# Layer norm statistics, router products and one input transform of a fused conv, attention and router kernel, rearranged in its first two stages

## The reference

```python
xn = _layernorm(x, axis=-1)                      # eps 1e-5, no weights
# attention branch
x = conv_general_dilated(xn, conv_w, 'SAME') + conv_b      # 3 taps, 4096 -> 3072
q, k, v = split(x, 3)                            # blocks of 128 tokens, 16 heads of 64
...                                              # causal softmax within a block
s = (o @ wo + bo) @ proj_w + proj_b
# router branch
scores = softmax(xn @ router_weight.T + router_bias)       # 64 experts
topk_w, topk_idx = top_k(scores, 8)
ffn = xn * topk_w.sum() + w_dense @ expert_bias
out = inputs + s * silu(ffn)
```

## Time and profile before

| | us |
|---|---|
| median of 3 runs | 1282.74 |
| range of the runs | 1281.09 to 1283.9 |
| profiled execution, its own time | 1284.49 |
| its span (slowest core, core 4) | 1283.0 |
| spans of the eight cores | 1272.1 to 1283.0 |
| PE busy in the span | 1089.1 |
| VectorE busy | 719.6 |
| ScalarE busy | 429.5 |
| GpSimd busy | 115.8 |

### The profile page before, as it was taken

The page is one execution under the profiler, slowest core; times in us unless marked ns, Lnnn a source line. Parts: engine busy times, 40 slices in busy tenths (PEclk is TensorE's granted clock), DMA queues, the critical chain, the costliest instruction groups (busy, mean ns, idle before and its releaser), DMA issues.

```text
span 1283.0 us, 15540 instructions; the slowest of 8 cores (1272.1 to 1283.0 us)
## 1 busy us (share of the span) xinstructions
PE 1089.1 (85%) x5200; PEld 493.9 (38%) x5200; DVE 719.6 (56%) x1140; ACT 429.5 (33%) x688; POOL 115.8 (9%) x128
## 2 busy tenths in 40 slices
PE   0119999999899998999999999999971555699997
PEld 0104444444344443444444444444430333433332
DVE  1877787677566525666665456666411444445454
ACT  1673333333233233333332433333212555322221
POOL 0002221000000000000000000000400000034544
PEclk9999999999899998999999999999995567799999
DMA  9910113667566548777776677777999000146765
GB/s 288 343 54 30 58 67 108 215 221 242 169 227 225 177 166 270 231 232 225 229 231 188 202 229 231 227 229 229 202 183 172 2 1 1 66 138 225 223 208 191
DMA packets 47943, 229.43 MB, mean 179 GB/s; under 512 B 6292, under 2 KB 6580, under 8 KB 44468
## 3 DMA queue, kind: packets, MB, share of 16 engines
q1 hardware_dynamic: 42872, 213.99, 52.8%
q0 software_dynamic: 3856, 13.27, 6.1%
q10 hardware_dynamic: 1136, 1.16, 0.3%
HBM read 222.79 MB, written 18.89 MB: 188 GB/s over the span
## 4 chain that ended last, share of the span: by engine, by line
PE 84%; DVE 7%; DMA 3%; issue 2%; another core or an unknown queue 2%; ACT 1%; ACTq 0%; POOLq 0%; DVEq 0%; SPq 0%
PE PS L202 80%; PE PS L206 4%; DVE AL L237 3%; DVE AL L209 2%; DMA AL<-rw 2%; DVE tNm L639 1%; DMA AL<-cw 1%; ACT AL L213 1%; ACTq L70 0%; DVE tMv L240 0%; ACT AL L215 0%; ACT tSd L213 0%; POOLq L804 0%; DVE tRr L658 0%
## 5 line engine op out<-in xcount | busy, mean ns | idle before, releaser
L202 PE MATMUL PS<-AL 128*128 128x512 bf16 (+4 forms) x4608 | 992.8, 379 | 20.6 <-DVE AL L209 15.2
L202 PEld LDWEIGHTS PS<-AL 128*128 128x128 bf16 (+3 forms) x4608 | 437.1, 102 | 551.9 <-issue 95.5
L209 DVE TENSOR_TENSOR AL<-AL 128x512 bf16<-128x512 f32 (+1 forms) x704 | 451.9, 687 | 265.8 <-PE PS L202 212.8
L213 ACT ACTIVATE AL<-AL 128x1024 bf16<-128x1024 f32 x193 | 203.4, 1054 | 426.9 <-PE PS L202 399.6
L206 PE MATMUL PS<-tI128f,AL 128*128 128x128 f32 (+3 forms) x304 | 43.2, 281 | 85.5 <-ACT AL L213 52.7
L209 POOL TENSOR_TENSOR AL<-AL 128x1024 f32<-128x1024 f32 x32 | 74.9, 2342 | 279.7 <-DVE AL L209 279.7
L213 ACT ACTIVATE AL<-PS 128x512 f32<-128x512 f32 (+2 forms) x88 | 56.5, 679 | 100.9 <-PE PS L206 77.2
L795 DVE SCALAR_TENSOR_TENSOR AL<-AL,tSc,PS 128x1024 f32<-128x1024 f32 x32 | 41.0, 1281 | 77.2 <-PE PS L202 77.2
L209 DVE TENSOR_TENSOR AL<-PS,AL 128x512 f32<-128x512 f32 (+1 forms) x80 | 71.9, 899 | 20.2 <-ACT AL L213 18.0
L206 PEld LDWEIGHTS PS<-tI128f,AL 128*128 128x128 f32 (+3 forms) x304 | 34.3, 152 | 109.1 <-issue 107.5
L213 ACT ACTIVATE AL<-AL,tScb 128x1024 f32<-128x1024 f32 x32 | 36.7, 1148 | 113.1 <-DVE AL L795 113.1
(11 more groups left out here) (52 smaller groups left out, 212.6 us busy)
## 6 DMA issues: line engine op xcount, KB each, us to landing
AL<-cw SPq DMA_DIRECT2D x192, 768.0 KB, 5.0
AL<-x SPq DMA_DIRECT2D x16, 1024.0 KB, 31.0
AL<-x SPq DMA_DIRECT2D x32, 512.0 KB, 4.9
out<-AL SPq DMA_DIRECT2D x32, 512.0 KB, 5.8
AL<-pw POOLq DMA_DIRECT2D x8, 1024.0 KB, 50.1
AL<-wq SPq DMA_DIRECT2D x8, 512.0 KB, 3.6
AL<-wk SPq DMA_DIRECT2D x8, 512.0 KB, 3.7
qhs<-AL SPq DMA_DIRECT2D x1, 2048.0 KB, 8.7
```

What stands on the lines that cost most here:

```text
L202: return PE.do(lambda e: e.matmul(out, lhsT, rhs, start=start, stop=stop, skip_group_check=skip), *toks, tok=tok)
L209: return eng.do(lambda e: e.tensor_tensor(out, a, b, op), *toks, tok=tok)
L213: return AC.do(lambda e: e.activation(out, in_, func, bias=bias, scale=scale), *toks, tok=tok)
```

## The change

It has five parts.

- **Loads.** The tiles are loaded in the order 0, 4, 1, 5, 2, 6, 3, 7, and the identity matrix has a semaphore of its own, so that the edge transposes no longer wait for the router weights.
- **Layer norm.** `ln_stats` is split into statistics, `ln_var` (aggregate and square root) and `ln_coef`. The square root of a tile is waited for only behind the first two `bn_stats` of the next tile. The square root is taken of 4(var + eps), so the reciprocal is `t_rh` itself and the halving is gone. The split of the projection bias, with its two DMAs on SyncE, stands behind the loop of stage 2.
- **Router.** The products of the odd tokens go to partitions 64 to 127 of the same bank instead of a bank of their own; the copy of the logits is one [128 x 512] instead of two [64 x 512], and its 8 transposes are 4 of 128 x 128.
- **Input transform.** Transform 0 of each chunk is made by GpSimd. Its token joins VectorE's in `k_v[c]`.
- **Conv units.** Pass 0 runs 4 matmuls in every step, from `st_` = 3, instead of 16 in every fourth; `prep` of unit g + 2 comes at `st_` = 4g + 3 instead of 4g + 5.

```diff
-        for t, d in ((t_i128f, d_i128), (t_cbT, d_cb), (t_bqT, d_bq), (t_bkT, d_bk),
+               for j in (0, 4, 1, 5, 2, 6, 3, 7)]
+        k_x = [k_x[i] for i in (0, 2, 4, 6, 1, 3, 5, 7)]
+        k_i128f = AC.dma(S("sC0"), t_i128f[:], d_i128)
...
+            return act(t_sd[rows, j:j + 1], t_mv[rows, 2 * j + 1:2 * j + 2], AF.Sqrt, k, k_eps,
+                       bias=t_eps[rows, :], scale=4.0)
+
+        def ln_coef(j, rows, k):
+            k = DV.do(lambda e: e.reciprocal(t_rh[rows, j:j + 1], t_sd[rows, j:j + 1]), k, tok=True)
...
-        k = act(t_pbh[:], t_pb[:], AF.Copy, k_c1)
-        k = tt(DV, t_pbl[:], t_pb[:], t_pbh[:], ALU.subtract, k)
-        SY.dma(S("sPB"), d_pbs[0], t_pbh[:], k)
-        k_pbs = SY.dma(S("sPB"), d_pbs[1], t_pbl[:])
-        k_edge = act(t_edge[:], PS[:, 0:64], AF.Identity, k_ed)
+                      k_xen, k_i128f, tok=(c == NCH - 1))
         all_r = slice(0, 128)
-        k_xn = []
-        for j in range(8):
-            k = ln_stats(j, xn[:, j, :], all_r, k_x[j])
-            k_xn.append(ln_apply(j, xn[:, j, :], all_r, k, 4))
+        k_xn = [None] * 8
+        k_sd = None
+        for i in range(8):
+            j = (i % 2) * 4 + i // 2
+            ln_stats(j, xn[:, j, :], all_r, k_x[j], 0, 2)
+            if i:
+                jp = ((i - 1) % 2) * 4 + (i - 1) // 2
+                k_xn[jp] = ln_apply(jp, xn[:, jp, :], all_r, ln_coef(jp, all_r, k_sd), 4)
+            k_sd = ln_var(j, all_r, ln_stats(j, xn[:, j, :], all_r, k_x[j], 2, 8))
+            if i == 1:
+                k_edge = act(t_edge[:], PS[:, 0:64], AF.Identity, k_ed)
+        k_xn[7] = ln_apply(7, xn[:, 7, :], all_r, ln_coef(7, all_r, k_sd), 4)
...
-                tt(DV, vout(3), h2(E0), h2(E1), ALU.subtract, k_p, tok=False)
-                k_v[c] = tt(DV, vout(0), h2(O0), h2(O1), ALU.subtract)
+                k_v0 = tt(GP, vout(0), h2(O0), h2(O1), ALU.subtract, k_ecopy, k_ocopy, k_p)
+                k_v[c] = (tt(DV, vout(3), h2(E0), h2(E1), ALU.subtract, k_p), k_v0)
...
-                mm(p_lg[:, 0:512], rwT[:, c, :], esb[i][:, 0:512], c == 0, c == NCH - 1,
-                   k_eo[c][0], k_c1)
-                k_rt[c] = mm(p_lg[:, 512:1024], rwT[:, c, :], osb[i][:, 1:513], c == 0, c == NCH - 1,
-                             k_eo[c][1], tok=True)
-                eo_free[i] = [k_v[c], k_rt[c]]
-            c = st_ - 2
-            if c >= 0 and c % 4 == 3:
-                g = c // 4
-                prep(g + LOOK)
-                k_pass[0] = conv_unit(g, 0, k_v)
+                mm(p_lg[0:64, :], rwT[:, c, :], esb[i][:, 0:512], c == 0, c == NCH - 1,
+                   k_eo[c][0], k_c1, skip=True)
+                k_rt[c] = mm(p_lg[64:128, :], rwT[:, c, :], osb[i][:, 1:513], c == 0, c == NCH - 1,
+                             k_eo[c][1], tok=True, skip=True)
+                eo_free[i] = [*k_v[c], k_rt[c]]
+            c = st_ - 3
+            if c >= 0:
+                if c % 4 == 0:
+                    prep(c // 4 + LOOK)
+                k_pass[0] = conv_unit(c // 4, 0, k_v, [c % 4])
...
-        k_lg = []
-        for h in range(2):
-            k_lg.append(DV.do(lambda e, h=h: e.tensor_scalar(
-                lgT[:, 512 * h:512 * h + 512], p_lg[:, 512 * h:512 * h + 512], 2.0, t_rbT[:],
-                ALU.mult, ALU.add), k_rt[NCH - 1], k_v[NCH - 1], tok=True))
-        k_lgfree = k_lg[1]
+        k = act(t_pbh[:], t_pb[:], AF.Copy, k_c1)
+        k = tt(DV, t_pbl[:], t_pb[:], t_pbh[:], ALU.subtract, k)
+        SY.dma(S("sPB"), d_pbs[0], t_pbh[:], k)
+        k_pbs = SY.dma(S("sPB"), d_pbs[1], t_pbl[:])
+
+
+        k_lgfree = DV.do(lambda e: e.tensor_scalar(lgT, p_lg, 2.0, t_rbT[:], ALU.mult, ALU.add),
+                         k_rt[NCH - 1], *k_v[NCH - 1], tok=True)
```

More of the change, by code:

```diff
@@ L99, in build_program @@
     d_pb = din("pb", [32, 128])
-    d_rb = din("rbT", [64, 1])
+    d_rb = din("rbT", [128, 1])
     d_i128 = din("i128", [128, 128])
@@ L166, in build_program @@
         osb = [f32v(B_KH + 4160 * i + 2080, 516) for i in range(2)]
-        lgT = f32v(B_KH, 1024, 64)
+        lgT = f32v(B_KH, 512)
         lgt = f32v(B_KH + 4096, 512)
@@ L220, in build_program @@
         k_x = [[SY.dma(S(f"sX{j}{h}"), xn[:, j, 2048 * h:2048 * h + 2048],
-                       d_x[j][:, 2048 * h:2048 * h + 2048]) for h in range(2)] for j in range(8)]
-        for t, d in ((t_i128f, d_i128), (t_cbT, d_cb), (t_bqT, d_bq), (t_bkT, d_bk),
+                       d_x[j][:, 2048 * h:2048 * h + 2048]) for h in range(2)]
+               for j in (0, 4, 1, 5, 2, 6, 3, 7)]
+        k_x = [k_x[i] for i in (0, 2, 4, 6, 1, 3, 5, 7)]
+        k_i128f = AC.dma(S("sC0"), t_i128f[:], d_i128)
+        for t, d in ((t_cbT, d_cb), (t_bqT, d_bq), (t_bkT, d_bk),
                      (t_bvT, d_bv), (t_boT, d_bo), (t_rbT, d_rb), (t_pb, d_pb)):
-            k_c1 = AC.dma(S("sC1"), t[:], d)
-        k_c1 = AC.dma(S("sC1"), rwT.rearrange("p c e -> p (c e)"), d_rw)
+            AC.dma(S("sC1"), t[:], d)
+        AC.dma(S("sC1"), rwT.rearrange("p c e -> p (c e)"), d_rw)
         k_c1 = (S("sC1"), S("sC1").n)
@@ L229, in build_program, with ln_stats @@
         k_c2 = (S("sC2"), S("sC2").n)
-        k_eps = DV.do(lambda e: e.memset(t_eps[:], EPS), tok=True)
-        def ln_stats(j, src, rows, loads):
+        k_eps = DV.do(lambda e: e.memset(t_eps[:], 4.0 * EPS), tok=True)
+        def ln_stats(j, src, rows, loads, c0, c1):
             s0 = 48 * j
             k = None
-            for c in range(8):
+            for c in range(c0, c1):
                 k = DV.do(lambda e, c=c: e.bn_stats(stats[rows, s0 + 6 * c:s0 + 6 * c + 6],
@@ L239, in ln_stats, with ln_var @@
                           loads[c * len(loads) // 8], tok=(c == 7))
+            return k
+        def ln_var(j, rows, k):
+            s0 = 48 * j
             k = DV.do(lambda e: e.bn_aggr(t_mv[rows, 2 * j:2 * j + 2], stats[rows, s0:s0 + 48]),
                       k, tok=True)
[L242 to L246, removed]
+            return act(t_sd[rows, j:j + 1], t_mv[rows, 2 * j + 1:2 * j + 2], AF.Sqrt, k, k_eps,
+                       bias=t_eps[rows, :], scale=4.0)
+        def ln_coef(j, rows, k):
+            k = DV.do(lambda e: e.reciprocal(t_rh[rows, j:j + 1], t_sd[rows, j:j + 1]), k, tok=True)
             return DV.do(lambda e: e.tensor_scalar(t_nmh[rows, j:j + 1], t_mv[rows, 2 * j:2 * j + 1],
@@ L260, in build_program @@
         r2 = slice(0, 2)
-        k = ln_stats(8, xe, r2, [k_xe])
-        k_xen = ln_apply(8, xe, r2, k, 1)[0]
+        k = ln_var(8, r2, ln_stats(8, xe, r2, [k_xe], 0, 8))
+        k_xen = ln_apply(8, xe, r2, ln_coef(8, r2, k), 1)[0]
         ed = PS[:, 0:64].rearrange("p (c s) -> p c s", c=NCH)
@@ L315, in dripped @@
                     drip.pop(0)()
-        p_lg = PS[0:64, 2048:3072]
+        p_lg = bank(4)
         bE, bO = bank(6), bank(7)
@@ L331, in h2, with conv_unit @@
             return a.rearrange("p (h f) -> p h f", h=2)
-        def conv_unit(n, setb, v_toks):
+        def conv_unit(n, setb, v_toks, ccs=range(4)):
             kind, p, g = stream[n]
@@ L337, in conv_unit @@
             k = None
-            for cc in range(4):
+            for cc in ccs:
                 c = 4 * g + cc
-                PE.wait(v_toks[c])
+                PE.wait(*v_toks[c])
                 for v in (1, 2, 3, 0):
@@ L344, in conv_unit @@
                            c == 0, c == NCH - 1, tok=(cc == 3 and v == 0))
-            u_free[u] = k
+            if 3 in ccs:
+                u_free[u] = k
             return k
@@ L413, in router_pe1 @@
             k = None
[L414 to L417, removed]
+            for j in range(4):
+                k = tr(pb_[:, 128 * j:128 * j + 128], lgT[:, 128 * j:128 * j + 128],
+                       t_i128f[:], k_lgfree, tok=(j == 3))
+            rd["k"] = DV.do(lambda e: e.tensor_copy(
+                lgt.rearrange("p (e j f) -> p j e f", e=2, j=4),
+                pb_.rearrange("p (j e f) -> p j e f", e=2, j=4)), k, tok=True)
             return rd["k"]
@@ L439, in r_keep @@
             k = tt(DV, t_wsum[:], ts8, rs8, ALU.mult, rd["k"])
-            k = tt(DV, t_sc[:], t_wsum[:], t_r[:, 0:8], ALU.mult, k)
+            k = DV.do(lambda e: e.scalar_tensor_tensor(t_sc[:], t_wsum[:], 2.0, t_rh[:, 0:8],
+                                                       ALU.mult, ALU.mult), k, tok=True)
             k = tt(DV, t_scb[:], t_sc[:], t_mv[:, 0:16:2], ALU.mult, k)
@@ L843, in _prep @@
         pb=cont(arr("L0_attn_proj_b").reshape(32, 128)),
-        rbT=cont(arr("L0_ffn_router_bias").reshape(64, 1)),
+        rbT=cont(np.tile(arr("L0_ffn_router_bias").reshape(64, 1), (2, 1))),
         i128=np.eye(128, dtype=f32),
```

4 lines of the change are left out of this document (1 added, 3 removed).

## The result

The changed kernel takes 1243.95 us (median, 1241.99 to 1244.83), the kernel before 1282.17 in the same runs: ratio 0.9698, 95% interval 0.9686 to 0.9711, 38.2 us less. The forecast was 1255 in 1243 to 1267, so the time lies at the fast edge of the range, nearer to the first rival (1246) than to the forecast. All times are medians over executions in which all eight cores ran at their usual granted clock (0.94 to 0.95 on the mean); in a few others half of the cores had 0.81 to 0.86, and those took over 1400 us.

A forecast was written before the change was run, and what follows sets the result against it. PE was taken to bound the kernel, after a VectorE-bound stage 1; in the changed loop VectorE with GpSimd. Stage 1's 23.3 us plus 5.3 from loop and handover (-7.4 + 2.1) gave 1254.1, forecast as 1255, range 1243 to 1267 (0.8).

The forecast's parts named there:

- the first rival: Steady loop: GpSimd and VectorE don't disturb each other, PE bounds at 3.3 us a step, 1246 us; chance 0.2.
- the prediction's own signs: Changed profile: prediction is wrong if the loop's step leaves 3.4 to 3.7 us or tiles land after 60 us.
- the later of the two limits: Stage 1: VectorE's eight tiles end at 59.3 us, loads plus four statistics at 60.5; the second ends last.
- the covered square root: Layer norm: the next tile's two statistics (1.2 us) cover the square root, even where it queues behind the normalising.
- even pass, even pass, odd pass, odd pass: only the second even and the first odd pass are neighbours: Router matmuls on PE: one of four passes is hidden, 0.45 us a step, so PE needs 3.3 us.
- the hold of 1.17 us: Steady loop: VectorE stands 1.17 us behind each GpSimd transform, middle of 1.08 to 1.26, giving 3.5 us a step.
- the sum (1254.1): Whole kernel: stage 1's 23.3 us plus loop and handover's 5.3 us, 28.6 us off, giving a median of 1254.1.
- unforeseen waits: Whole kernel: small waits only add, so the forecast was put at 1255 instead of 1254.1.
- a gap of 1 to 2 us ahead of pass 1 and 0.5 at unit 10: Handover: PE waits 1 to 2 us for the logits' copy; stores ahead of unit 10's loads cost 0.5 us more.

The follow-up runs named there:

- c_rw: The changed kernel with the router weights (1 MB) loaded on SyncE's queue behind the tiles instead of beside them: 1243.36 us, ratio 0.9691.
- b_bias: The kernel before with only the bias split moved behind stage 2's loop and the edge copy behind the tiles: 1262.75 us, ratio 0.9850.
- b_ln: The kernel before with all of the changed stage 1 and nothing of stage 2: 1264.26 us, ratio 0.9843.
- a_rser: The changed kernel with both router products on the first 64 columns and banks of their own, as before: 1263.55 us, ratio 0.9840.
- e_read: The changed kernel with GpSimd's transform on VectorE, edge copies on ScalarE, plus an unused two-input GpSimd read (f32 output) every step: 1272.19 us, ratio 0.9923.
- e_readb: The changed kernel with GpSimd's transform on VectorE, edge copies on ScalarE, plus an unused two-input GpSimd read (bf16 output) every step: 1270.51 us, ratio 0.9907.
- A: The changed kernel itself, with all five parts, against the kernel before: 1243.95 us, ratio 0.9698.

## Why the prediction was right or wrong

The time lies within the range, but by the prediction's own signs its working failed in two sizes: a step of 3.10 is outside of 3.4 to 3.7, and the last aggregate came at 64.10 instead of 60 to 61. The two errors have opposite signs, and only the width of the range, which was drawn to take in the first rival, covers what is left. That part was luck.

**Stage 1: right in its mechanism, 2 us too much.** VectorE started on tile 0 at 11.9 us, as said. (What held it before was not the bias split alone: the edge copy waited for the same weights.) The term that was mis-sized is "the later of the two limits": VectorE's 5.9 us a tile and the loads' 6.1 (2.1 MB at 345 GB/s) are so close that a late half costs time that is not made up. VectorE waited 6.7 us for halves; with 1 MB less ahead of them (c_rw) it waited 4.6 and ended earlier. The last product came at 64 to 66 instead of 62.0: 21 us instead of 23.3, and in the eight other kernels with this stage 1 the loop starts 19 us earlier. What I gave the moved statistics credit for, the covered square root, is worth nothing that can be measured (0.9850 in b_bias, 0.9843 in b_ln, and starts of 75.1 and 73.9, within the spread of equal stages).

**PE's step: wrong.** The step "even pass, even pass, odd pass, odd pass: only the second even and the first odd pass are neighbours" took the order of the instructions for the order of their four records. The records start in pairs; 0.85 to 0.9 us a step is hidden, not 0.45, and PE needs 2.85 instead of 3.3. The Trainium skill (TensorEngine Tiling (Array Packing), Theoretical Speedup), which gives up to twice the throughput, was right here, and I gave it too little weight. The error did not enter the forecast, since PE was not to be the bound. It would have mattered with the right hold: at 3.10 for the pair of VectorE and GpSimd, a PE of 3.3 would have set the step.

**VectorE with GpSimd: right mechanism, hold too large.** This pair sets the loop, as forecast. The term that was mis-sized is the hold of 1.17 us, the time that VectorE loses for each transform of GpSimd: 4 x 3.10 less 9.3 (12 x 0.60 + 2.1) is 3.1, or 0.77 for each transform. The step is 3.10 instead of 3.5, and the loop gives 0.64 x 31 = 20 us before the handover instead of 7.4. Less the 2.3 us of stage 1, that is the 10 us by which the sum (1254.1) was too slow; the eleventh is what the forecast of 1255 had added for unforeseen waits. In a_rser the same transform costs VectorE (77.13 - 93 x 0.60)/24 = 0.89, a read of other data 1.07 (e_read). All three rest on 0.60 for an operation of VectorE, and are good to about 0.1. Why the real transform is the cheapest was not found; the type of its output isn't it (e_readb).

**The first rival** (GpSimd and VectorE don't disturb each other, 1246) came nearest in number, with a mechanism that is shown false: the step was not PE's, PE waited, and taking GpSimd out gained 7 us.

**The handover: right in its mechanism.** Forecast were a gap of 1 to 2 us ahead of pass 1 and 0.5 at unit 10; 1.79 and, on the mean of the cores, 0.8 were there (1.38 on core 6). The first load behind the stores took 5.9 us to land instead of 5.2.

**The sum.** On the mean of the cores: -21.0 for the start and -15.9 from there to attention, against -36.9 in the spans. The time, that of the slowest core, fell by 38.2; the 1.3 us between lie in the spread of the cores, of the wait at attention above all.

## What to carry to other kernels

Before work goes from VectorE to GpSimd, look at what both read: if VectorE's operations take two tensors from SBUF and GpSimd's reads SBUF, they hold each other up, and the move can give back all that it takes away; here the loop is shorter without it (2.86 us a step against 3.10). Ask of an early instruction that waits for a whole group of loads whether anything behind it is held up for no reason; here two tiny operations, one on VectorE and one on ScalarE, were worth 20 us, and the elaborate pipelining beside them nothing that could be measured. And follow an operation that is moved through the DMA queues as well: two stores of 8 KB held the loads of three units' weights back.

## What the runs showed of the hardware beyond that

- Two f32 products with 64 output partitions each, on different halves of the array's columns, take together about the time of one: 1.86 - (3.70 - 2.85) = 1.0 us instead of 1.86 (a_rser against A; they also share a bank there), although each is a single instruction that runs as two records, and the two stand one behind the other in PE's list.
- A GpSimd copy of one column can be held up for several VectorE operations in a row: 3.46 us for 0.18 us of work. In the kernel before, where VectorE was busy for 84.43 of 108 us, it never took more than 0.67.
- GpSimd fills of 128 x 512 f32, three in each step, beside a VectorE that was busy for 78.86 of 80 us left its operation at 683 ns.
